# Cross-attention by pairs of heads: 64-row score tiles, another order of the turned banks, and half as many key copies

## The reference, cut to what matters

```python
q = split_heads(norm(x) @ Wq + bq)            # 16 heads x 128 x 16
k = split_heads(ctx @ Wk + bk)                # 16 heads x 12544 x 16
v = split_heads(ctx @ Wv + bv)
scores = einsum('hqd,hkd->hqk', q, k) * 16 ** -0.5 + mask
attn = softmax(scores)                        # over 12544 keys
x = x + merge_heads(einsum('hqk,hkd->hqd', attn, v)) @ Wo + bo
```

## Time and profile before

| | us |
|---|---|
| three runs, median | 1845.32 (1844.47 to 1846.0) |
| the profiled execution | 1845.17 |
| its span, first to last instruction | 1843.4 |
| TensorE busy | 1623.4, 88% of the span |
| VectorE busy | 1068.7, 58% |
| ScalarE busy | 900.1, 49% |

### The profile page before, as it was taken

The page is one execution under the profiler, slowest core; times in us unless marked ns, Lnnn a source line. Parts: engine busy times, 40 slices in busy tenths (PEclk is TensorE's granted clock), DMA queues, the critical chain, the costliest instruction groups (busy, mean ns, idle before and its releaser), DMA issues.

```text
span 1843.4 us, 34030 instructions
## 1 busy us (share of the span) xinstructions
PE 1623.4 (88%) x13482; PEld 1237.0 (67%) x13482; DVE 1068.7 (58%) x1958; ACT 900.1 (49%) x1439; POOL 15.1 (1%) x23
## 2 busy tenths in 40 slices
PE   0597997458999999999997797999999999999499
PEld 0365476236787878888785465788878788888356
DVE  6422322447677777777785325777767777777322
ACT  0011031003777777767785120776677676778221
POOL 0000000100000000000000000000000000000000
PEclk9799988669999999999998798999999999999599
DMA  8356754127654555656332175665635446550354
GB/s 351 115 185 198 265 140 128 83 114 157 144 141 101 121 120 125 143 125 151 81 82 81 61 284 121 153 145 124 159 82 141 101 121 139 125 120 2 137 234 179
DMA packets 42811, 257.09 MB, mean 139 GB/s; under 512 B 9929, under 2 KB 10185, under 8 KB 33993
## 3 DMA queue, kind: packets, MB, share of 16 engines
q1 hardware_dynamic: 42664, 255.05, 50.0%
HBM read 152.12 MB, written 0.13 MB: 83 GB/s over the span
## 4 chain that ended last, share of the span: by engine, by line
PE 81%; DMA 7%; DVE 7%; SPq 2%; ACT 2%; issue 2%; POOL 1%; POOLq 0%; DVEq 0%; ACTq 0%
PE T L534 16%; PE O L635 12%; PE S L611 10%; PE S L539 7%; PE O L534 7%; PE T L586 6%; PE T L599 5%; PE O L697 4%; PE O L586 3%; PE O L599 3%; PE S L814 2%; DMA ctx_in<-in_ctx_cols 2%; DMA wide<-in_ctx_rows 2%; PE O L847 2%; DMA wide<-in_up_L0f 2%
## 5 line engine op out<-in xcount | busy, mean ns | idle before, releaser
L1224 DVE CUSTOM_DVE_ANT_0 sc<-S,mask_bias,small 128x896 f32<-128x896 f32 x448 | 513.3, 1146 | 181.6 <-PE S L611 180.5
L926 ACT ACTIVATE sc<-sc,small 128x1792 f32<-128x1792 f32 x224 | 399.6, 1784 | 0.0
L534 PE MATMUL T<-consts,sc 128*128 128x128 f32 (+1 forms) x2200 | 336.3, 277 | 8.8 <-ACT sc L1015 6.4
L534 PEld LDWEIGHTS T<-consts,sc 128*128 128x128 f32 (+1 forms) x2200 | 260.7, 141 | 83.4 <-issue 49.3
L912 ACT ACTIVATE pT<-T 128x512 f32<-128x512 f32 (+1 forms) x446 | 232.0, 523 | 160.3 <-PE T L534 160.3
L611 PE MATMUL S<-keys,q 128*128 128x512 f32 (+1 forms) x896 | 291.8, 407 | 1.4 <-DMA keys<-keys_hl 1.4
L635 PE MATMUL O<-pT,arena 128*32 128x128 f32 x6272 | 238.8, 276 | 0.0
L635 PEld LDWEIGHTS O<-pT,arena 128*32 128x32 f32 x6272 | 179.1, 109 | 37.4 <-issue 37.2
L534 PE MATMUL O<-consts,sc 128*128 128x128 f32 x1048 | 166.7, 276 | 0.0
L912 ACT ACTIVATE pT<-O 128x512 f32<-128x512 f32 (+1 forms) x226 | 118.0, 522 | 84.6 <-PE O L534 84.6
L534 PEld LDWEIGHTS O<-consts,sc 128*128 128x128 f32 x1048 | 125.1, 140 | 35.0 <-issue 24.2
(11 more groups left out here) (281 smaller groups left out, 1453.0 us busy)
## 6 DMA issues: line engine op xcount, KB each, us to landing
keys<-keys_hl SPq DMA_DIRECT2D x448, 224.0 KB, 5.7
ctx_in<-in_ctx_cols SPq DMA_DIRECT2D x42, 896.0 KB, 7.3
wide<-in_up_L3f SPq DMA_DIRECT2D x8, 2048.0 KB, 9.0
wide<-in_ctx_rows SPq DMA_DIRECT2D x14, 896.0 KB, 5.5
wide<-in_up_L0f SPq DMA_DIRECT2D x8, 1408.0 KB, 9.3
sc<-in_ctx_cols SPq DMA_DIRECT2D x10, 896.0 KB, 7.9
wide<-in_up_L2f SPq DMA_DIRECT2D x8, 1024.0 KB, 6.6
wide<-in_down_L2f SPq DMA_DIRECT2D x8, 1024.0 KB, 4.8
```

What stands on the lines that cost most here:

```text
L534: last = nc.tensor.transpose(out[0:w, t * P:(t + 1) * P], src[:, t * w:(t + 1) * w], ident)
L926: nc.scalar.activation(sc[:, n % 3, :], sc[:, n % 3, :], ACT.Exp, bias=n_best[c % 2][:, h:h + 1], scale=-1.0, accum_out=l_new[c % 2][:, h: ...
L1224: V.tensor_tensor_reduce(sc[:, n % 3, i * HC:(i + 1) * HC], S4f[:, i * 2 * BANK:i * 2 * BANK + HC], mask_bias[:, i * HC:(i + 1) * HC], 1.0 ...
```

## The change

Two heads are now worked on together (`m` counts pairs, 56 in a layer).

- **Scores.** A head has 64 rows of its own (four places of 16), and the two heads of a pair lie at rows 0 to 63 and 64 to 127. `scores(m, half)` issues four matmuls of 64 rows, the two heads in turn, into all four banks of `S4`. It waits until all four banks of the half before were taken.
- **Turned banks.** The 28 blocks of a pair fill 7 full banks. VectorE empties banks 0, 1 and 6, ScalarE 2, 3, 4 and 5. `pT2` is held once for a pair, and `weights_of` adds a fourth buffer to `sc`.
- **Order.** On TensorE: turn 0, 1; scores of the next pair, first half; turn 2, 3; a projection; turn 4; the turned sums (every second pair); scores of the next pair, second half; turn 5, 6; a projection; then `multiply(m)` at once, with 56 instructions. Before, a head's product came behind the turning of the next head.
- **Projections.** `PROJECTED` has two units behind each pair but the last, which has one.
- **Key copies.** 8 transfers per half, each with 64 rows of source and 16 rows of destination for four pairs, the same bytes in all. The columns of Wk are put in another order for it. The loads of the next context wait for other units.
- **Queries.** `q4` is made by a copy and two subtractions on 32 rows, without the masked products.

```diff
@@ PROJECTED @@
-PROJECTED = {1: [("V", 0)], 2: [("V", 1)], 3: [("V", 2)],
-             4: [("K", 0, 0)], 5: [("K", 0, 1)], 6: [("K", 0, 2)], 7: [("K", 0, 3)],
-             8: [("V", 3)], 9: [("V", 4)], 10: [("V", 5)],
-             11: [("K", 1, 0)], 12: [("K", 1, 1)], 13: [("K", 1, 2)], 14: [("K", 1, 3)], 15: [("V", 6)]}
+PROJECTED = {0: [("V", 0), ("V", 1)], 1: [("K", 0, 0), ("V", 2)], 2: [("K", 0, 1), ("K", 0, 2)],
+             3: [("K", 0, 3), ("V", 3)], 4: [("V", 4), ("V", 5)], 5: [("K", 1, 0), ("V", 6)],
+             6: [("K", 1, 1), ("K", 1, 2)], 7: [("K", 1, 3)]}
@@ emptied_by @@
-    return "act" if u[0] == "T" and u[2] != 1 else "dve"
+    return "act" if u[0] == "T" and u[2] not in (0, 1, TURNS - 1) else "dve"
@@ load_keys @@
-                            sp.wait_ge(s["s_ready"], 2 * (H * (c - 1) + HH * (hf + 1)))
-                        for r in range(4):
-                            for j in range(HH // 2):
-                                sp.dma_start(keys4[QR * r:QR * (r + 1), hf * HH // 2 + j, :].bitcast(F32),
-                                             keys_hl[QR * j:QR * (j + 1), r % 2, :].bitcast(F32)) \
+                            sp.wait_ge(s["s_ready"], 2 * (NP * (c - 1) + NP // 2 * (hf + 1)))
+                        for head in range(2):
+                            for r in range(4):
+                                at = HR * head + DH * r
+                                sp.dma_start(keys4[at:at + DH, hf * HH // 2:(hf + 1) * HH // 2, :].bitcast(F32),
+                                             keys_hl[HR * head:HR * (head + 1), r % 2, :].bitcast(F32)) \
                                     .then_inc(s[f"keys_in{hf}"], 16)
@@ scores @@
-                    if n:
-                        pe.wait_ge(s["s_taken"], 2 * (n - 1) + half + 1)
+                    if m or half:
+
+                        pe.wait_ge(s["s_taken"], 4 * m + 2 * half)
                     for n0, n1 in ((0, BANK), (BANK, HC)):
-                        last = mm(S4f[:, half * 2 * BANK + n0:half * 2 * BANK + n1], q4[:, h, :],
-                                  keys4[:, h // 2, half * HC + n0:half * HC + n1], start=True, stop=True)
+                        for i in range(2):
+                            own = slice(HR * i, HR * (i + 1))
+                            last = mm(S4f[:, i * 2 * BANK + n0:i * 2 * BANK + n1], q4[own, j, :],
+                                      keys4[own, j, half * HC + n0:half * HC + n1], start=True, stop=True)
@@ multiply @@
+                    pe.wait_ge(s["t_dve"], emptied(("T", m, TURNS - 1)))
+                    pe.wait_ge(s["t_act"], emptied(("T", m, TURNS - 2)))
+                    for t in range(2 * TB):
+                        i, b = divmod(t, TB)
+                        g = t % 4
+                        at = (2 * (m % 2) + i) * P
+                        last = mm(O2[32 * g:32 * g + 32, 1, at:at + P], vv[:, c % 2, b, j * 32:(j + 1) * 32],
+                                  pT2[:, t * P:(t + 1) * P], start=(b < 4), stop=(b >= TB - 4))
@@ TensorE's order @@
+                for m in range(PAIRS):
+                    turn(m, 0)
+                    turn(m, 1)
+                    if m + 1 < PAIRS:
+                        scores(m + 1, 0)
+                    turn(m, 2)
+                    turn(m, 3)
+                    project(m, 0)
+                    turn(m, 4)
+                    if quad_turned(m) is not None:
+                        turn_quad(quad_turned(m))
+                    if m + 1 < PAIRS:
+                        scores(m + 1, 1)
+                    for g in range(5, TURNS):
+                        turn(m, g)
+                    project(m, 1)
+                    multiply(m)
@@ ScalarE's order @@
+                for m in range(PAIRS):
+                    if quad_turned(m) is not None:
+                        take_quad(quad_turned(m))
+                    take_turned(m, 2)
+                    take_turned(m, 3)
+                    project(m, 0)
+                    take_turned(m, 4)
+                    take_turned(m, 5)
+                    if m + 1 < PAIRS:
+                        soften(2 * m + 2)
+                    project(m, 1)
+                    if m + 1 < PAIRS:
+                        soften(2 * m + 3)
@@ VectorE's order @@
+                for m in range(PAIRS):
+                    c, j = divmod(m, NP)
+                    take_turned(m, 0)
+                    take_turned(m, 1)
+                    if m + 1 < PAIRS:
+                        for n in range(2):
+                            take_scores(2 * m + 2 + n, 0)
+                    project(m, 0)
+                    if quad_turned(m) is not None:
+                        take_quad(quad_turned(m))
+                    if m + 1 < PAIRS:
+                        take_scores(2 * m + 2, 1)
+                    take_turned(m, TURNS - 1)
+                    if m + 1 < PAIRS:
+                        take_scores(2 * m + 3, 1)
+                    project(m, 1)
```

More of the change, by code:

```diff
@@ L144, in unit_order @@
     units += [("K", 0, 1, nb) for nb in range(KEY_UNITS)]
[L145 to L150, removed]
+    for m in range(PAIRS):
+        units += [("T", m, g) for g in range(4)] + [projected(m, 0), ("T", m, 4)]
+        if quad_turned(m) is not None:
+            units.append(("O", quad_turned(m)))
+        units += [("T", m, g) for g in range(5, TURNS)] + [projected(m, 1)]
+    units.append(("O", PAIRS // 2 - 1))
+    return [u for u in units if u]
 UNITS = unit_order()
@@ L194, in build @@
         slots = [max(sum(PACKS[n].values()) for n in LAYERS[i::2]) for i in range(2)]
-        packs = [sb("packs0", [P, slots[0]])]
-        packs1_at = nc.sbuf_base
-        packs.append(sb("packs1", [P, slots[1]]))
+        packs = [sb(f"packs{i}", [P, slots[i]]) for i in range(2)]
+        packs1_used = max(sum(PACKS[n].values()) for n in ("L2a", "L3x", "L3f"))
+        assert packs1_used + CH <= slots[1]
         arena_at = nc.sbuf_base
@@ L224, in build, with weights_of @@
         keys4 = nc.alloc_sbuf_tensor_at("keys4", [P, NP, CH], F32R, offset=wide_at)
[L225 to L229, removed]
+        q4 = nc.alloc_sbuf_tensor_at("q4", [P, NP, P], F32R, offset=work_at + 4 * BANK)
+        sc_last = packs[1][:, packs1_used:packs1_used + CH]
+        def weights_of(n):
+            return sc[:, n % 4, :] if n % 4 < 3 else sc_last
         def ring(u):
@@ L457, in load_next_ctx @@
                             return
[L458 to L462, removed]
+                        sp.wait_ge(s["t_ready"], UNIT_AT["K", c, 1, 2 * half + 1] + 1)
                         load_ctx(s[f"ctx_in{half}"], 2 * c + 2 + half, half)
@@ L601, in value_unit, with scores @@
                     last.then_inc(s["t_ready"], 1)
[L603 to L607, removed]
[L608 to L609 removed]
+                def scores(m, half):
+                    c, j = divmod(m, NP)
+                    if half == 0 and j % (NP // 2) == 0:
+                        pe.wait_ge(s[f"keys_in{j // (NP // 2)}"], KEY_COPIES * 16 * (c + 1))
+                    if m or half:
+                        pe.wait_ge(s["s_taken"], 4 * m + 2 * half)
@@ L624, in multiply @@
-                def multiply(n):
-                    c, h = divmod(n, H)
-                    if h == 0:
-                        pe.wait_ge(s["t_dve"], emptied(("V", c, VALUE_UNITS - 1)))
[L629 to L637, removed]
-                                  start=(b < 4), stop=(b >= TB - 4))
+                    for t in range(4):
+                        i, b = divmod(4 * g + t, TB)
+                        last = nc.tensor.transpose(ring(u)[:, t * P:(t + 1) * P],
+                                                   weights_of(2 * m + i)[:, b * P:(b + 1) * P], ident)
@@ L1261, in cross @@
                 need(dve, "pe", f"{layer}.qT_ps")
-                def queries(ap, rows):
-                    n = rows.stop - rows.start
-                    return ap.rearrange("p (j n) -> p j n", n=P).unsqueeze(2).to_broadcast([n, NP, 2, P])
-                def own_rows(rows):
-                    n = rows.stop - rows.start
-                    return C["pair"][rows, :].unsqueeze(1).unsqueeze(3).to_broadcast([n, NP, 2, P])
-                upper, lower = slice(0, P // 2), slice(P // 2, P)
-                qT = S4f[:, 0:2 * BANK]
-                V.tensor_tensor(q4[upper].rearrange("p (j a) n -> p j a n", a=2), queries(qT[upper], upper),
-                                own_rows(upper), ALU.mult)
-                link(V.tensor_copy(q_up[lower], qT[lower]))
-                link(V.tensor_tensor(q_low[lower], qT[lower], q_up[lower].bitcast(F32), ALU.subtract))
-                done("dve", V.tensor_tensor(q4[lower].rearrange("p (j a) n -> p j a n", a=2),
-                                            queries(q_low[lower], lower), own_rows(lower), ALU.mult), f"{layer}.q4")
+                qT = S4f[:, 0:NP * P]
+                q4f = q4[:, :, :].rearrange("p j n -> p (j n)")
```

(8 more changed lines are left out.)

185 lines of the change are left out of this document (86 added, 99 removed).

## The result

The changed kernel takes **2330.65 us** (median of 4 runs, 2327.32 to 2334.39) against 1844.89 for the kernel before on the same chip: ratio 1.2633, 95% interval 1.2611 to 1.2655. Forecast were 1857 us and a range of 1820 to 2070. The sign was right; the time lies 50 us above the one that was worked out for the rival "Copies to 16 rows are slower" in full (2280 us, chance 0.14).

A forecast was written before the change was run, and what follows sets the result against it. The prediction took TensorE's issue to bound the kernel, with no wait costing anything. Chunks with projections -32, last chunk +20, key copies +24 and queries and start 0 sum to +12: 1845.2 + 12 = 1857 us, range 1820 to 2070.

The forecast's parts named there:

- The sign: Whole kernel: slower than before, 1857 us against 1845.3, +0.6%; chance of slower 0.65.
- Copies to 16 rows are slower: Rival on the key copies: rate halves to 102 GB/s, 2280 us, chance 0.14; slowed in part, 1880 to 2070, chance 0.20.
- Key copies: Copies of a half as fast as before, 19.7 us; ScalarE waits 0.8 and 1.2 us, +24 us in all.
- product visit, 56 instructions and the blocks behind: TensorE's product, one visit per pair of heads: 2.06 us instead of 2.30, a gain of 0.24 a pair.
- score visit: stream and switch: TensorE's four 64-row score matmuls: 0.44 us side by side plus 0.24 for changing tile shape, against 0.82 before.
- chunk with projections: Chunk of 16 heads: -4.2 + 1.3 + 0.2 = -2.7 us from 81.9; 12 chunks give -32 us.
- pair of the last chunk: Pair without projections: TensorE and VectorE wait for each other around bank 6, +1.45 us on 7.20; +20 us over 14 pairs.
- start of a layer, to the third key copy: Queries and first scores at a layer's start: savings hidden by the wait for key copies, 0 us.
- slack of a copy: Time free for a half's key copies before ScalarE's next upper part needs their end: 18.7 and 18.3 us.
- The layout by hand: Pair with two key units laid out on the engines: TensorE dense, 9.50 us for 10.0, spare times 0.2 to 0.3 us.
- no switch cost: Rival on score visits: changing tile shape costs nothing, pair about 9.1 us, 1819 us in all, chance 0.18.
- the two heads' scores do not run side by side: Rival on score visits: heads' matmuls run in turn, +0.38 us a half, +73 us, 1930 us, chance 0.06.

The follow-up runs named there:

- runs 3 and 4: Kernel before, each 32-row key copy cut into two of 16 neighbouring rows: 2177.37 us; changed kernel, each key copy cut by columns into two, 16 rows kept: 2331.39 us.
- run 2: Changed kernel with four key copies per half, each writing 32 rows four apart over all 128, queries laid out to match: 1806.5 us, ratio 0.981.
- run 11: Kernel with rows four apart, each copy cut by heads into transfers of 16 rows, one head's issued before the other's: 1877.04 us, ratio 1.0189.
- runs 9 and 10: Kernel with rows four apart, each score visit's four matmuls issued twice: heads in turn 1890.79 us, head after head 1893.44 us.
- runs 7, 9 and 10: The first: kernel with rows four apart, score matmuls issued head after head instead of in turn, 1814.7 us; the others: see runs 9 and 10.
- run 1: Changed kernel with each key copy's 16 destination rows two apart, spread over 32 rows, same transfers and bytes: 1914.89 us, ratio 1.0389.

## Why the prediction was wrong, step by step

**The step that failed** is the term "Key copies": "This takes the copies to be as fast as before, with the same bytes in 8 transfers", 19.7 us a half and +24 us. Measured are 35.0 us (34.2 to 35.3 over both layers), a wait of 17.8 and a cost of 18.8 where 0.8 and 1.2 were forecast. The reason that I gave against the rival, the wider source and the fewer transfers, is worth nothing by runs 3 and 4. The rows to judge by were there, 204 GB/s to 32 rows and 400 to 128; I wrote that the rate falls with the rows, and then gave the full fall 0.14.

**What the term is worth.** The kernel with rows four apart differs from the changed one in the copies and in how the queries are laid out for them. Between the two spans lie 528 us. A chunk is 116.3 against 78.7, 37.6 more for two waits: the copies of 35.0 and 35.2 outlast their slacks of 18.5 and 17.9 by 16.5 and 17.3, and the low clock adds 2.0 and 1.7, 37.5 in all. So each of the 24 waits costs 18.8, and 24 x 18.8 = 451. From first to third key copy L2x takes 106.1 against 58.3 us and L3x 104.0 against 57.9; less one wait in each, 29 and 27 are left. In L2x 23.6 of the 29 are the first copies, which stand bare on the chain (34.7 us against 11.1), and 5.4 come from the second copies, whose slack is not 18.5 but 13.1 (440.48 to 453.58 in run 2). That makes 507; the other 21 us lie in the last chunks and between the layers and were not traced further.

The rival's own working, 26 x 16.3 on 1857, had the excess of a copy about right. That it came within 50 us is luck in part: it missed the low clock, about 2 us in each of 24 waits, and the larger loss at the start of the layers, and it stood on a sum of the other terms that was some 27 us too high (1833 for the kernel without waits, which takes 1806.5).

**The other terms**, read where no copy is in the way (the kernel with rows four apart, and pairs between the waits of the changed one):

| step | predicted | measured |
|---|---|---|
| product visit, 56 instructions and the blocks behind | 2.06 | 1.67 + 0.15 = 1.82 |
| score visit: stream and switch | 0.44 + 0.24 = 0.68 | 0.41 + 0.34 = 0.75 |
| pair with two key units and turned sums | 9.50 + 0.44 = 9.94 | 9.87 |
| chunk with projections | 81.9 - 2.7 = 79.2 | 78.68 |
| pair of the last chunk | 8.65 | 8.40, 8.44 in the changed kernel |
| last chunk, L2x | +10 | +9.0 (116.8 against 107.8) |
| start of a layer, to the third key copy | 0 | +7.7 with copies as fast as before (run 11, 75.5 against 67.8), -9.4 with those of run 2 (58.3) |
| slack of a copy | 18.7 and 18.3 | 18.5 and 17.9 |
| all, copies without waits | 1833 | 1806.5 |

The dense pair of the changed kernel, between two waits, from the end of one product to that of the next:

```profile
743.17 1.03 PE T L631 x8
744.20 0.60 PE S L617 x4
...
751.38 1.67 PE O L648 x56
753.04 0.59 PE T L631 x4
```

The layout by hand held: a chunk came within 0.5 us and the last chunk's pair within 0.25, where TensorE waits for VectorE's bank 6 as forecast. The errors of the two visits cancel in part: the product is 0.24 cheaper and the two score visits 0.14 dearer. The product was read from the earlier trace rows, where the old order stands: in its trace four product instructions start every 0.11 us, but the last four of each head start two by two, so two heads take 16 such steps, and the new numbering over both heads takes 14. The rival "no switch cost" is refuted by runs 9 and 10, and "the two heads' scores do not run side by side" by runs 7, 9 and 10; with the copies of run 2 the time fell on the faster side all the same, for the start of the layers (2 x 9.4) and the chunks.

The forecast was low even on its own assumption. Run 11 has copies about as fast as before (19.3 us, then 19.4 to 20.8) and takes 1877 us, not 1857. In a chunk its copies of 19.7 and 19.6 us outlast the slacks of 18.5 and 17.9 by 2.9 in all, and the chunk is 81.74 - 78.68 = 3.1 longer, 1.5 a wait and not 1.0: the slacks were sized 0.2 and 0.4 too long, and the 0.17 to spare wasn't there. The rest lies at the start of the layers, which was put at nothing: to the third key copy run 11 takes 7.7 us more than the kernel before in L2x and 6.5 in L3x (73.7 against 67.2), where ScalarE's longest waits lie, 8.2 and 7.4 us, for the second copies of a layer, whose slack was not laid out. No low clock follows the waits in a chunk of run 11 (granted 1.00). In run 1 it does: copies of 20.4 and 21.0 us outlast the slacks by 5.0 in all, and 1.6 more come from one slow value unit and product, which makes 6.6 of the chunk's 85.36 - 78.68 = 6.7.

## What to carry to other kernels

Price a copy between rows of SBUF by where the rows stand that each transfer writes, before bytes or count: here laying out operands so that every transfer writes rows spread over all 128 turned a kernel 26% slower into one 2% faster, with the same arithmetic. When a change narrows a transfer's rows and the transfer has a deadline, work out the slack against the slow rate first, and give a rate that two rows of the profile bracket its full weight. Work out the slack of every copy, the first ones of a layer too: the second copies had 13.1 us here where the later ones had 18. And a transfer that misses its slack by enough costs more than the miss: TensorE came back at the low clock after each wait of some 17 us and after 13 of 24 waits of some 4, but not after those of a chunk in run 11.

## What was unexpected of the hardware

After a stall of 17 us TensorE does its next value unit in 3.23 us and not 1.73, at 0.85 of granted clock over the chunk; with rows two apart, where ScalarE's waits are 4.0 us in the mean, the same unit takes 1.73 after 11 of them and 2.78 to 3.41 after 13, and the chunk's clock is 0.98. Eight transfers in flight to different rows don't add their rates: 16 rows four apart with the heads in turn reach 200 GB/s, transfers over both heads' rows 330. And four score matmuls of 64 rows cost 0.42 us more in either order of the heads, side by side both times, while going in and out of 64-row tiles costs 0.34 us, more than the 0.24 that I had taken from the products.
